# First-tile order and the place of the query and key turns in an attention layer with a running output, on one core

## The reference, cut to what matters

```python
q = einsum('bsd,ed->bse', x, Wq); k = ...Wk; v = ...Wv      # 32 query heads, 8 key heads, D = 128
q, k = rope(rmsnorm(q, q_w), pos), rope(rmsnorm(k, k_w), pos)
k_all = concat([k_cache[block_table], k]); v_all = ...       # 512 cached + 32 new keys
scores = where(valid, q @ k_all^T * SCALE, -1e30)
x = x + (softmax(scores) @ v_all) @ Wo^T
logits = x @ Wr^T + 5 * one_hot(language); gates = softmax over the two highest
x = x + x @ W^T + 2 * sum over experts of gate * (x @ A^T) @ B^T
```

## Time and profile before

| | |
|---|---|
| median of three runs | 1481.78 us |
| the profiled execution: its time, its span | 1482.79 us, 1481.0 us |
| mean granted TensorE clock | 0.965 |
| PE, weight loads, DVE, ACT, POOL busy | 90%, 81%, 69%, 55%, 61% |
| DMA | 207.11 MB, mean 140 GB/s |

### The profile page before, as it was taken

How to read it: one execution, slowest core, us unless ns; L and a number is a source line. 1 busy time by engine, 2 the same in 40 slices (tenths; PEclk the granted TensorE clock), 3 DMA queues, 4 the chain that set the end, 5 groups by cost and what they waited for, 6 DMA issues and landing times. The chain is left out here.

```text
span 1481.0 us, 29026 instructions
## 1 busy us (share of the span) xinstructions
PE 1328.8 (90%) x8896; PEld 1201.2 (81%) x8896; DVE 1021.0 (69%) x2555; ACT 814.0 (55%) x2091; POOL 898.9 (61%) x1101
## 2 busy tenths in 40 slices
PE   3789999998889999998988999999888999999999
PEld 2678888987778988887877888888778898888887
DVE  5677777676587666677667676766768766666754
ACT  3555556555565555556555555555556655555641
POOL 5666766656766666676556775666677566666600
PEclk8899999999999999999999999999999999999999
DMA  4664344445544444445545434444555444444421
GB/s 161 212 182 143 114 136 123 130 137 175 156 146 149 120 135 132 142 117 175 151 125 184 139 115 126 134 124 144 175 154 168 130 133 130 130 141 135 132 78 57
DMA packets 73252, 207.11 MB, mean 140 GB/s; under 512 B 12176, under 2 KB 12464, under 8 KB 73008
## 3 DMA queue, kind: packets, MB, share of 16 engines
q0 software_dynamic: 40960, 134.25, 31.8%
q1 hardware_dynamic: 31392, 69.53, 14.6%
q10 hardware_dynamic: 816, 2.29, 0.5%
HBM read 195.77 MB, written 12.36 MB: 141 GB/s over the span
## 5 line engine op out<-in xcount | busy, mean ns | idle before, releaser
L1086 POOL DMA_INDIRECT kv_rows<-in_kv,step_idx x512 | 522.8, 1021 | 196.4 <-issue 139.9
L665 ACT ACTIVATE soft<-soft,min_all 128x544 f32<-128x544 f32 x256 | 191.9, 750 | 368.6 <-DVE min_all L848 365.9
L461 PE MATMUL O<-pT,kv_rows 128*128 128x128 f32 x2048 | 285.8, 285 | 4.2 <-ACT pT L661 3.5
L848 DVE CUSTOM_DVE_ANT_0 soft<-SX,mask 128x544 f32<-128x544 f32 x256 | 184.8, 722 | 148.8 <-PE SX L181 148.3
L461 PEld LDWEIGHTS O<-pT,kv_rows 128*128 128x128 f32 x2048 | 272.9, 201 | 16.9 <-ACT pT L661 6.4
L661 ACT ACTIVATE pT<-PT 128x640 f32<-128x640 f32 x256 | 179.2, 700 | 189.3 <-PE PT L450 184.7
L181 PE MATMUL SX<-kT,qT_hi 128*128 128x288 f32 (+1 forms) x1024 | 227.2, 311 | 52.5 <-DVE qT_lo L894 48.7
L1109 POOL TENSOR_TENSOR rope_u<-rope_u,rope_v 128x512 f32<-128x512 f32 (+1 forms) x96 | 105.5, 1099 | 277.9 <-DVE rope_v L829 276.4
L181 PEld LDWEIGHTS SX<-kT,qT_hi 128*128 128x128 f32 x1024 | 166.0, 194 | 62.6 <-DVE qT_lo L894 58.4
L870 DVE TENSOR_TENSOR kT<-KT,kT 128x512 fp32r<-128x512 f32 x256 | 175.4, 685 | 5.8 <-ACT kT L643 5.5
L409 PE MATMUL KT<-ident,kv_rows 128*128 128x128 f32 x1024 | 158.1, 278 | 13.1 <-DMA kv_rows<-in_kv,step_idx 8.7
(11 more groups left out here) (203 smaller groups left out, 2463.3 us busy)
## 6 DMA issues: line engine op xcount, KB each, us to landing
mask<-mask_rows SPq DMA_DIRECT2D x64, 272.0 KB, 3.7
stage<-in_wqkv SPq DMA_DIRECT2D x22, 512.0 KB, 4.4
x_raw<-in_xT SPq DMA_DIRECT2D x32, 256.0 KB, 4.5
kv_rows<-in_kv,step_idx POOLq DMA_INDIRECT x512, 3.7
stage<-in_wo SPq DMA_DIRECT2D x16, 512.0 KB, 3.8
y_tile<-y_running SPq DMA_DIRECT2D x32, 256.0 KB, 3.2
y_running<-y_tile SPq DMA_DIRECT2D x31, 256.0 KB, 3.0
out<-kv_rows SPq DMA_DIRECT2D x8, 256.0 KB, 2.0
```

The lines of the kernel that those rows point to most:

```text
L461: nc.tensor.matmul(O[:, 0:P], kv_rows[:, b, c, GK * D + h * D:GK * D + (h + 1) * D], pT[:, c * P:(c + 1) * P], start=c == 0, stop=False)
L665: nc.scalar.activation(probs[:, p % 2, 0:KEYS], scores[:, p % 2, :], ACT.Exp, bias=min_all[:, p:p + 1], scale=-1.0, accum_out=den[:, p:p + ...
L848: V.tensor_tensor_reduce(scores[:, p % 2, :], SX[:, SX_AT:SX_AT + KEYS], mask[:, b, :], 1.0, BIG, ALU.add, ALU.min, min_all[:, p:p + 1]).t ...
L1086: G.indirect_dma_start(kv_rows[:, b, c, :], None, kv[:, :], bass.IndirectOffsetOnAxis(ap=step_idx[:, b * LC + c:b * LC + c + 1], axis=0)). ...
```

## The change

In the loop: q_rot gets a buffer for each head. The new keys are turned in pair 3 instead of 5, into MISC instead of PROJ, and taken by ACT and DVE in pair 3 too. The query of head 0 is turned in pair 5 instead of 4. The query of head 1 is turned behind the weigh of pair 6 instead of ahead of it; ACT and DVE take it at the head of pair 7 instead of within pair 6. The waits follow: `turn_q` of head 0 waits for the new keys to be taken out of MISC, that of head 1 for PROJ, and POOL's q_rot for the turn of the same head one tile earlier.

In the first tile: ACT rounds x, POOL makes the mask row behind the first gather, DVE makes the sum and q_rot of head 0, POOL makes only rstd for it; the orders of all engines change as the diff shows.

```diff
-        q_rot = sb("q_rot", [P, 512])
+        q_rot = sb("q_rot", [P, GK, 512])
-        K_NEW = PROJ[:, 0:GK * P]
+        K_NEW = MISC[:, 0:GK * P]
...
-            def turn_k(i, blocks):
+            def turn_k(i):
                 pe.wait_ge(sm["rot_ready"], i * NBLK + 1)
-                pe.wait_ge(sm["raw_ready"], i * NBLK + blocks)
...
             def turn_q(i, h):
                 pe.wait_ge(sm["rot_ready"], i * NBLK + 2 + h)
+                if h == 0:
+                    pe.wait_ge(sm["kT_new_ready"], i + 1)
+                else:
+                    pe.wait_ge(sm["raw_ready"], i * NBLK + NBLK)
...
             for half in halves:
                 proj(0, 0, half, 0)
-            turn_keys(0, 0)
             for half in halves:
                 proj(0, 1, half, 0)
-            turn_k(0, 2)
+            turn_keys(0, 0)
+            turn_k(0)
+            proj(0, 2, halves[0], 0)
+            turn_q(0, 0)
             turn_keys(0, 1)
-            turn_q(0, 0)
-            proj(0, 2, halves[0], 0, True)
             score(0, 0)
...
-                    if not last and p == 4:
+                    if not last and p == 3:
                         pe.wait_ge(sm["y_added"], CREDIT + i)
+                        turn_k(i + 1)
+                    if not last and p == 5:
                         turn_q(i + 1, 0)
-                    if not last and p == 5:
-                        turn_k(i + 1, NBLK)
+                    weigh(i, p)
                     if not last and p == 6:
                         turn_q(i + 1, 1)
-                    weigh(i, p)
...
(ACT, first tile)
+            act.wait_ge(sm["xT_in"], 16)
+            nc.scalar.activation(x_hi[:, :, :], x_raw[:, :, :], ACT.Copy).then_inc(sm["x_hi_ready"], 1)
             startup_block(0, 32, lambda half: stage[:, half, :, :])
...
-            take_kT(0, 0)
             take_block(0, 1)
             square_block(0, 1)
+            take_kT(0, 0)
             take_kT_new(0)
-            take_kT(0, 1)
             startup_block(2, 48, lambda half: stage[:, half, :, :])
             take_qT(0, 0)
+            take_kT(0, 1)
...
(ACT, loop)
+                    if not last and p == PAIRS - 1:
+                        take_qT(i + 1, 1)
                     take_pT(i, p)
...
+                    if not last and p == 3:
+                        take_kT_new(i + 1)
                     if not last and p == 5:
                         take_qT(i + 1, 0)
-                        take_kT_new(i + 1)
...
-                    if not last and p == 6:
-                        take_qT(i + 1, 1)
...
(DVE, first tile: mask instructions out, to POOL; split_x without its copy)
             mean_square(0, 0)
-            rest_kT(0, 0)
             rotate(0, 1)
             mean_square(0, 1)
+            V.tensor_tensor(rope_u, rope_u, rope_v, ALU.add)
+            V.tensor_tensor(q_rot[:, 0, :], rope_u, rstd, ALU.mult)
+            rest_kT(0, 0)
             rest_kT_new(0)
             fill_slots(0, 0)
-            rest_kT(0, 1)
             startup_rest(2, lambda half: stage[:, half, :, :])
             rest_qT(0, 0)
+            rest_kT(0, 1)
...
(DVE, loop)
+                    if not last and p == PAIRS - 1:
+                        rest_qT(i + 1, 1)
                     if p + 1 < PAIRS:
                         normalise(i, p + 1)
...
+                        if p == 3:
+                            rest_kT_new(i + 1)
                         if p == 5:
                             rest_qT(i + 1, 0)
-                            rest_kT_new(i + 1)
                             fill_slots(i + 1, 0)
-                        if p == 6:
-                            rest_qT(i + 1, 1)
...
(POOL)
-                    pool.wait_ge(sm["q_turned"], i * GK + k - 1)
-                    dst = q_rot[:, :]
+                    if not (isinstance(i, int) and i == 0):
+                        pool.wait_ge(sm["q_turned"], i * GK + k - 2)
+                    dst = q_rot[:, k - 1, :]
...
             gather(0, 0, LC)
+            (the mask row: copy, memset, compare)
             G.memset(v_own[:, :, :], 0.0).then_inc(sm["v_zero"], 1)
             rotate_sum(0, 0)
-            rotate_sum(0, 1)
+            make_rstd(0, 1)
             gather(1, 0, LC)
```

More of the change, by code:

```diff
@@ L384, in _, with proj @@
             xs = lambda c: (x_hi[:, c, :], x_lo[:, c, :])
-            def proj(i, k, part, wcount, new_keys_first=False):
+            def proj(i, k, part, wcount):
                 first, n = part
@@ L944, in _ @@
             mean_square(0, 0)
-            rest_kT(0, 0)
             rotate(0, 1)
             mean_square(0, 1)
+            dve.wait_ge(sm["uv_ready"], 2)
+            V.tensor_tensor(rope_u[:, :], rope_u[:, :], rope_v[:, :], ALU.add).then_inc(sm["sum_ready"], 1)
+            dve.wait_ge(sm["sum_ready"], 2)
+            dve.wait_ge(sm["pow_ready"], 2)
+            dve.wait_ge(sm["rot_ready"], 1)
+            V.tensor_tensor(q_rot[:, 0, :].rearrange("p (r d) -> p r d", d=D), rope_u[:, :].rearrange("p (r d) -> p r d", d=D),
+                            rstd[:, :].rearrange("p (r a) -> p r a", a=1).to_broadcast([P, REP, D]), ALU.mult
+                            ).then_inc(sm["rot_ready"], 1)
+            rest_kT(0, 0)
             rest_kT_new(0)
             fill_slots(0, 0)
-            rest_kT(0, 1)
             startup_rest(2, lambda half: stage[:, half, :, :])
             rest_qT(0, 0)
+            rest_kT(0, 1)
             dve.wait_ge(sm["w_lo_ready"], 4)
@@ L1101, in make_table, with make_rstd @@
                     G.tensor_tensor(dst, a, w, ALU.mult).then_inc(sm["table_ready"], 1)
+            def make_rstd(i, k):
+                n = GK if k == 0 else REP
+                pool.wait_ge(sm["ms_ready"], i * NBLK + k + 1)
+                G.tensor_tensor(rstd[:, 0:n], meansq[:, k, 0:n], minus_half[:, 0:n], ALU.pow).then_inc(sm["pow_ready"], 1)
             def rotate_sum(i, k):
@@ L1109, in rotate_sum @@
                 G.tensor_tensor(rope_u[:, 0:w], rope_u[:, 0:w], rope_v[:, 0:w], ALU.add).then_inc(sm["sum_ready"], 1)
-                pool.wait_ge(sm["ms_ready"], nth)
-                G.tensor_tensor(rstd[:, 0:n], meansq[:, k, 0:n], minus_half[:, 0:n], ALU.pow).then_inc(sm["pow_ready"], 1)
+                make_rstd(i, k)
                 pool.wait_ge(sm["sum_ready"], nth)
@@ L1134, in _ @@
             gather(0, 0, LC)
+            pool.wait_ge(sm["row_in"], 16)
+            pool.wait_ge(sm["iota_ready"], 2 + ROWS)
+            G.tensor_copy(row_f[:, :], row_i[:, :]).then_inc(sm["row_ready"], 1)
+            pool.wait_ge(sm["row_ready"], 1)
+            mask_row = y_tile.bitcast(BF16)[0:BATCH, 0:KEYS]
+            G.memset(mask_row[:, L:KEYS], 0.0).then_inc(sm["row_ready"], 1)
+            pool.wait_ge(sm["row_ready"], 2)
+            G.tensor_scalar(mask_row[:, 0:L], key_index[0:BATCH, :], row_f[:, 0:1], BIG, ALU.is_ge, ALU.mult
+                            ).then_inc(sm["mask_made"], 1)
             G.memset(v_own[:, :, :], 0.0).then_inc(sm["v_zero"], 1)
             rotate_sum(0, 0)
-            rotate_sum(0, 1)
+            make_rstd(0, 1)
             gather(1, 0, LC)
```

17 lines of the change are left out of this document (4 added, 13 removed).

## The result

The changed kernel takes **1427.2 us** (median of four runs, 1425.7 to 1430.7) where the kernel before takes 1482.65 in the same comparison: a ratio of 0.9619, 95% interval 0.958 to 0.9658, so 3.8% faster. The forecast was 1436. The profiled execution has a span of 1423.9 us for 1481.0.

A forecast was written before the change was run, and what follows sets the result against it. Bound: a chain of PE work, with DVE behind POOL's addition and POOL's own chain close. Gains 7 x 1.54 + 16 x 0.7 + 5 x 2.8 + 3 x 1.5 = 40.5 us, plus 6 in the first tile: 1436 us, range 1392 to 1457.

The forecast's parts named there:

- The bound and the chain: At each tile boundary, PE, DVE behind POOL's addition and POOL's own chain are three limits close together.
- the held case: Mean square still held to the addition's end: score 0.44 us sooner, product 1.54 sooner at full clock, 0.7 at reduced; chance 0.45.
- DVE then reaches the mean square at some 648.7 ... 0.6 us ahead: At the common boundary, DVE starts the second block's mean square some 0.6 us ahead of POOL's addition, not 0.27.
- new keys two pairs sooner: New keys' turn and takes move from pair 5 to 3, so their 0.44 us no longer stands before the copy into the slots.
- None has escaped yet: Argument against the mean square running free of POOL's addition: leads of 0.27 and 0.39 us were both held.
- Sixteen clock losses taken as given: 16 of 22 boundaries with a 1.9 to 2.1 us pause before the score lose clock; counted at 0.7 us gain each, 11.2.
- The late q_rot: Five boundaries where PE waits 2.1 to 2.9 us for q_rot: turn hidden, gain 2.8 us each, 14.0 in all.
- The split weights: Three boundaries where weights are split: only the oT_lo pause is won, 1.5 us each, 4.5 in all.
- The first tile: Reordered start: third block turned at some 42 instead of 48.30; gain between 3 and 8 us, taken as 6.
- A: Rival: the mean square escapes POOL's addition, score 1.16 us sooner, pause 1.4 us, clock kept; 1400 us, chance 0.33.
- B: Rival: the wait before the score only moves to another held VectorE instruction, score starts as now; 1452 us, chance 0.12.
- C: Rival: moved DVE instructions hold POOL's chain, up to 1.06 us on each of three rstd a tile; 1535 us, chance 0.05.

The follow-up runs named there:

- the kernels with pauses of 1.56, 1.27 and 1.0 us: Changed kernel with, in turn: query of head 0 turned in pair 4 (1418.2 us); four memsets before POOL's addition (1404.8); mean square ahead of the keys' rest (1398.6).
- the memsets on POOL: Changed kernel with four one-column memsets ahead of POOL's addition for the second query block, nothing else moved: 1404.8 us, ratio 0.9499.
- the kernel in which it is made to happen: Changed kernel with VectorE's mean square of the second query block put ahead of the turned keys' rest in pair 5: 1398.6 us, ratio 0.9421.

## Why the prediction was right, and where not

**The bound and the chain**: right. The score stands behind the addition through the mean square, and the held case is what happened: the score 0.93 behind the addition instead of 1.42, so 0.49 sooner (forecast 0.44); the product 3.61 us behind the score at full clock (3.60) and 4.87 to 4.92 at reduced clock (4.98); the copy inside the rstd, unheld. Measured from the end of POOL's addition, the product of a common boundary comes 1.56 to 1.58 us sooner where both kernels have full clock (1.54), and 0.8 to 1.0 where both have lost it (0.7). Putting back the second turn costs 42 us, so this was the part that carried the change, and its two reasons, the takes ahead of take_o and the wait on q_rot, each show by themselves. The parts don't add up, though: undone one by one in the changed kernel they are worth 42, -18, -9 and 0 of the 55 us.

**"DVE then reaches the mean square at some 648.7 ... 0.6 us ahead"**: wrong. The lead is 0.40. The working let the new keys' rest in pair 3 delay DVE by 0.33 and minimum 7 come 0.3 sooner, so that the two nearly cancelled. But the second block's rotation comes 0.54 us later against the addition than in the kernel before, DVE has no wait left in front of minimum 7, and the minimum starts only 0.1 sooner against it. With the new keys back in pair 5 the lead is 0.93. So "new keys two pairs sooner", from which the forecast had its 0.44 us, cost 18.

**"None has escaped yet"** left out a row of the kernel before. A mean square at 31.73 in the first tile, 0.20 us ahead of the addition of 31.93, took its plain time:

```profile
31.73 0.17 DVE L836 TENSOR_SCALAR meansq<-sumsq 128x4 f32<-128x4 f32 x1
```

There POOL had stood idle for 8.24 us before the addition. In all the held ones the addition comes straight behind a gather.

**Sixteen clock losses taken as given**: the mis-sized term. I argued that the pause stays at about 2.1 us, since PE would get through the turned keys 0.47 sooner, just as the score. It got there only 0.22 sooner (0.40 behind the start of the addition, at 625.23, where before it was 0.62, at 649.92), while the score came 0.49 sooner. So the pause went to 1.80, and eleven of the sixteen boundaries kept the clock: the sixteen gave 25.0 us instead of 11.2. The kernels with pauses of 1.56, 1.27 and 1.0 us, in which no common boundary loses it, bear out that the clock goes with the pause, if not with it alone (the kernel before with the mean square sooner). Why PE gained only 0.22 I did not find.

**The late q_rot**: 13.8 us for 14.0, and by the path that was forecast, though with a hold that my working left out. The mean square escapes, and the copy behind it starts 0.43 us ahead of the addition and is held:

```profile
881.65 0.15 DVE L841 TENSOR_SCALAR meansq<-sumsq 128x4 f32<-128x4 f32 x1
...
882.32 1.87 DVE L891 CAST kT<-k_new 128x256 fp32r<-128x256 f32 x1
...
882.75 1.28 POOL L1121 TENSOR_TENSOR rope_u<-rope_u,rope_v 128x512 f32<-128x512 f32 x1
...
884.29 0.50 PE L181 MATMUL SX<-kT,qT_hi 128*128 128x288 f32 x2 [1.85 <-issue]
886.59 0.66 PE L424 MATMUL PROJ<-ident,q_rot 128*128 128x128 f32 x4 [0.20 <-POOL q_rot L1132]
```

That hold costs next to nothing, since the second turn waits for q_rot all the same: where the memsets on POOL let the copy through, the score comes 1.5 us sooner against the addition's end and the product still 3.9 us behind it, as here. Measured from that end the product comes 2.7 us sooner than before at three of the five (2.8), 3.1 at one, and 1.5 at the one that lost its clock. The split weights gave 3.9 us for 4.5.

**The first tile**: the second turn came 3.8 us sooner than in the earlier trace rows and not 6, and PE still waits 5.17 us for it. The first rotation on DVE waited 2.42 us for the mask on POOL (timelines of PE and DVE of the changed kernel):

```profile
44.48 1.11 PE L424 MATMUL PROJ<-ident,q_rot 128*128 128x128 f32 x4 [5.17 <-POOL q_rot L1132]
...
20.98 0.43 DVE L829 TENSOR_TENSOR rope_u<-raw,table 128x256 f32<-128x256 f32 x1 [2.42 <-POOL y_tile L1155]
```

At the first output product the gain is 6.3 us, for 6 and 1.5 in the forecast; at the end the reorder is worth nothing that these runs can tell (1426.75 without it). So of the five terms the clock's was 13.8 us too small and the others together 3.3 too large. That 1436 lies only 9 us off owes those 3.3 to luck, and not more.

**The rivals.** A, the escape, did not happen in the changed kernel, but its price was right: 1400 forecast, and the kernel in which it is made to happen takes 1398.6. The Trainium skill (SBUF — State Buffer, section Who interferes with whom) says that whoever issues first has the shared ports for the whole instruction. The traces agree at recorded leads of 0.66 us and more. At leads up to 0.63 behind a gather they do not, the second comer holds the first: 0.14 in the kernel with the query in pair 4 (619.99 against 620.13), 0.27, 0.40 and 0.60 in others. The leads are between the starts that the profile records; whether GpSimd has the ports before its recorded start, no row shows. The same section says that a VectorE instruction with one SBUF input outside the two-port modes does not contend; qT_lo, whose other input is in PSUM, agrees. B and C did not show: the score moved, and the median rstd is 1.05 us as before.

**Open**: what the gather ahead of the addition has to do with the hold; what q_rot's second buffer is worth, which no run undid; what lets the changed kernel's first tile give back its lead in the tiles behind it, and what makes one pause of 1.80 lose the clock and the next keep it.

## What to carry to other kernels

Where two engines contend, don't ask only whether an instruction overlaps, but which of the cheap ones is caught, and how many steps stand between it and the one that the critical engine waits for: a 0.16 us instruction, one place sooner, was worth 2%, and 0.15 us more work on the other engine over 1%. Before a step is moved, write down what it passes: the new keys moved sooner took nothing from PE and cost 18 us by what stood behind them on DVE. And undo a change part by part even when it is a success; two parts of this one were a loss (18 and 9 us) and one was worth nothing.

## What the runs showed of the hardware

A VectorE mean square (SBUF to SBUF, 128x4) that starts shortly ahead of GpSimd's 128x512 addition is held to the end of it when the addition comes straight behind a gather. In the fourteen traces there are 471 such with recorded leads of 0.02 to 0.63 us, and all took 1.34 us or more, up to 1.95; 164 with 0.66 to 1.26, and all took 0.15 to 0.23. With a memset directly ahead of the addition none of 27 was held, at leads from 0.21 us, and none of three where GpSimd had stood idle before the addition, at 0.19 and 0.20. A copy of 128x256 was held at leads up to 0.45 (1.87 us for 0.28) and took 0.28 at 0.84 to 0.87. A held VectorE copy that reaches into GpSimd's next instruction goes with a longer rstd, mostly 1.38 to 1.41 us for 1.05.

The granted clock: after a pause of 1.87 to 2.08 us 16 of 22 boundaries fell from 1.00 to 0.72 over the next six microseconds, which is the 1.2 GHz level for part of it; after 1.80 us 6 of 19; after 1.55 to 1.62 us, 1.27 and 1.0 none of those that I counted (some 20 in each of four kernels). The pause before the score is not the whole of it: with 0.9 us there and a wait of 1.4 us for q_rot behind it, 7 of 31 lost it. A loss cost 1.3 us a tile in the changed kernel and 0.5 in the kernel before, where waits elsewhere in the tile grew shorter with it (4.70 to 5.22 from score to product).
